# Two-layer conditioned residual block on one core: the first and the last linear stage take two chunks in a matmul of 512 columns

## The chip, the core and the metric

The kernel runs on one core of a Trainium2 chip. The metric is the device time of one execution in microseconds (us), lower is better. The engines that matter here are PE (TensorE, matmul), ACT (ScalarE), DVE (VectorE) and POOL (GpSimd); SP (SyncE) issues nearly all DMA transfers. Each engine works its own instructions strictly in the order of the program, and they wait for each other by semaphores alone.

## What is computed

`x` has 8 batches of 1024 tokens with 512 features, all in float32. Cut to what matters, with a style vector per batch (s0, sk, so) made from `cond_512` at the start:

```python
y  = ((x * s0) @ W0.T) * demod0 + b0          # layer L0, 512 x 512
x1 = x + clip(y, -256, 256)
kx = ((x1 * sk) @ Wk.T) * demodk + bk         # layer K
# attention of the 16 heads of one token with each other: a 16 x 16 matrix per token, q = k = v = kx
k  = kx.reshape(B, N, 16, 32)
A  = softmax(einsum('bnhd,bnjd->bnhj', k, k) / sqrt(32))
a  = einsum('bnhj,bnjd->bnhd', A, k).reshape(B, N, 512)
out = x1 + ((a * so) @ Wo.T) * demodo + bo    # layer O
```

## The kernel before

The 8192 tokens are cut into N = 32 chunks of T = 256 tokens. Features lie on the partitions (KB = 4 blocks of 128), tokens along the free axis. Everything is written out by hand in Bass: each engine's list of steps is a table, and the order in the table is the order of execution.

For a chunk c the steps are these. ACT and DVE split the scaled input into a high and a low part in fp32r (`x_hi_of` on ACT, 2 halves of 2 instructions; `x_lo_of` on DVE, the same). PE forms **L0** in 4 blocks m of 128 output features; each block is 12 matmuls (4 k, times w_hi·hi, w_hi·lo, w_lo·hi) into one of NLB = 4 PSUM banks. ACT evacuates a block (`l0_out`: demodulation and bias). DVE clips and adds x (`make_x1`, in halves). `x1_hi_of`, `x1_lo_of` split x1, PE forms **K**, `k_out` evacuates it to `kx`. SP writes kx to DRAM and reads it back turned (`k_to_dram`, then `k_from_dram`, 4 issues), DVE reorders it (`turn_k`, tile `k_rhs`), POOL (3 groups) and ACT (`copy_keys`) spread it into `k_bd`, and PE forms **scores**. For the values SP writes `k_rhs` to DRAM (`v_to_dram`) and reads it turned (`v_from_dram`, 4 issues, tile `k_v`); DVE transposes it (`turn_v`). Softmax alternates: ACT `even_scores`, DVE `merge_scores`, `subtract_maxima`, ACT `exponentials`, DVE `sums`, `normalise`; then DVE (`spread_probabilities`) and ACT (`spread_some`, 4 instructions) spread the probabilities and PE forms **pv**. ACT copies the result out of PSUM (`evacuate_y`), SP turns it through DRAM (`y_to_dram`, 4 issues, then `y_from_dram`, tile `yr`), ACT and DVE split it (`y_hi_of`, `y_lo_of`), PE forms **O**, ACT evacuates it (`o_out`), DVE adds x1 (`finish`), SP stores it (`store`).

The steps are software-pipelined. A head fills the pipeline (chunks 0 to 5), a loop runs i = 6 to 29, a tail empties it. In a turn of the loop PE does L0 of chunk i, O of i-4, K of i, pv of i-2 and scores of i-1, in this order (L179); ACT, DVE and SP have tables of their own for a turn (L654, L850, L341). A linear block waits for the evacuation of the block four before it (L414). SP's queue is in order too: a transfer that waits holds up all transfers behind it.

Of the kernel before, what the change touches and what calls it, by code (L numbers as in the profile page):

```python
# [34 lines left out]
def build(nc, xT, condT, wT, affT, aff_b, lin_b, block_ones, token_mask, head_diag, dim_eye, outT):  # L35
# [33 lines left out]
    with ExitStack() as ctx:  # L69
# [27 lines left out]
        x_hi, x_lo = sb("x_hi", [KB, T], F32R), sb("x_lo", [KB, T], F32R)  # L97
# [15 lines left out]
        y_hi, y_lo = sb("y_hi", [2, KB, T], F32R), sb("y_lo", [2, KB, T], F32R)  # L113
        o_sb = sb("o", [2, KB, T])
# [64 lines left out]
        def pe_steps(i):  # L179
            return blocks(L0, i) + blocks(O, i - 4) + blocks(K, i) + one("pv", i - 2) + one("scores", i - 1)  # L180
# [34 lines left out]
        def _(sp):  # L215
# [71 lines left out]
            def store(c, h, parts):  # L287
# [118 lines left out]
        def _(pe):  # L406
            operands = {L0: (x_hi, x_lo), K: (x1_hi, x1_lo)}
            split = {L0: (a_xhi, v_xlo), K: (a_x1hi, v_x1lo), O: (a_yhi, v_ylo)}

            def linear(l, c, m, width=1):  # L410
# [101 lines left out]
        def _(act):  # L512
            evacuated = []

            def evacuate(l, c, m, out):
# [21 lines left out]
            def x_hi_of(c, h):  # L537
# [4 lines left out]
                if c >= 2:  # L542
                    act.wait_ge(pe_lin, done(L0, c - 1 if c > 2 else 0, KB - 1))
                hi_part(L0, c, h, y_hi[:, 1] if c == 1 else x_hi, x_sb[:, c % 2], a_xhi)
# [387 lines left out]
```

## Time and profile before

| what | value |
|---|---|
| time, median of 3 runs (lowest, highest) | 707.4 us (705.88, 712.59) |
| the profiled execution | 707.48 us, of which its span is 705.6 us |
| busy in the span: PE / DVE / ACT / POOL | 690.7 / 580.8 / 545.0 / 116.3 us (98 / 82 / 77 / 16%) |
| chain that ended last, by engine | PE 76%, ACT 8%, DVE 7%, DMA 4%, issue 3%, SP 2% |
| DMA | 140.39 MB, mean 199 GB/s |

The page gives busy time by engine; the chain of waits says what the end of the span waited for; the timeline gives instructions with their start, so that the distance from one start to the next is what an instruction costs its engine when nothing waits. "Idle before" names the engine that ended a wait.

### The profile page before, as it was taken

The numbers are of one execution on the slowest core, as the hardware profiler recorded it, in microseconds if no ns is written. First come the engines' busy times: TensorE is split into PE (matmuls) and PEld (weight loads), VectorE is DVE, ScalarE is ACT, GpSimd is POOL, SyncE is SP. The second block draws the span as 40 slices with busy tenths as digits, with TensorE's granted clock in tenths as the row PEclk, the third lists the DMA queues.
The fourth block names the chain that finished last, engine by engine and source line by source line (L and its number), as shares of the span: only waits on it lengthen the run. The fifth ranks groups of instructions, "written<-read, shape, count | busy, mean of one in ns | idle before, by whom it ended". The sixth has DMA issues, their size and how long they took to land.

```text
span 705.6 us, 21755 instructions
## 1 busy us (share of the span) xinstructions
PE 690.7 (98%) x8944; PEld 674.6 (96%) x8944; DVE 580.8 (82%) x1048; ACT 545.0 (77%) x1072; POOL 116.3 (16%) x107
## 2 busy tenths in 40 slices
PE   9999999999999999999999999999999999999877
PEld 8999999999999999999999999999999999999877
DVE  4689988889888889988889878888988889878853
ACT  6898977888777888777787867788777788877743
POOL 2021301111101111110111101111110111112200
PEclk9999999999999999999999999999999999999989
DMA  8367867678877777886667785777876777878853
GB/s 294 126 181 199 218 184 198 193 210 212 210 186 199 201 205 223 214 213 182 190 201 207 209 227 133 206 203 215 217 205 173 208 200 206 210 188 220 218 155 120
DMA packets 229700, 140.39 MB, mean 199 GB/s; under 512 B 141281, under 2 KB 223201, under 8 KB 229601
## 3 DMA queue, kind: packets, MB, share of 16 engines
q1 hardware_dynamic: 228544, 138.73, 72.2%
q8 instruction: 71, 1.16, 0.7%
q10 hardware_dynamic: 1056, 0.26, 0.2%
q14 instruction: 29, 0.23, 0.1%
HBM read 71.85 MB, written 67.11 MB: 197 GB/s over the span
## 4 chain that ended last, share of the span: by engine, by line
PE 76%; ACT 8%; DVE 7%; DMA 4%; issue 3%; SPq 2%; POOL 0%; ACTq 0%; DVEq 0%
PE lin_ps L429 61%; PE y_ps L501 7%; PE s_ps L483 6%; ACT p_bd L628 2%; DMA yr<-y_turned 1%; ACT x_hi L534 1%; ACT kx L525 1%; ACT y_hi L534 1%; PE s_ps L439 1%; ACT o L525 1%; SPq L273 1%; DVE x L803 1%; DMA k_v<-v_turned 1%; DVE sc L833 1%; ACT sc L622 1%
## 5 line engine op out<-in xcount | busy, mean ns | idle before, releaser
L429 PE MATMUL lin_ps<-x_hi,w_hi 128*128 128x256 f32 x1008 | 286.4, 285 | 0.3
L429 PE MATMUL lin_ps<-x_lo,w_hi 128*128 128x256 f32 x1008 | 281.4, 280 | 0.9 <-issue 0.9
L429 PE MATMUL lin_ps<-x_hi,w_lo 128*128 128x256 f32 x1008 | 281.2, 280 | 0.0
L398 POOL COPY k_bd<-k_rhs 32x1024 f32<-32x1024 f32 x96 | 111.9, 1166 | 547.5 <-DVE k_rhs L782 543.8
L429 PEld LDWEIGHTS lin_ps<-x_hi,w_hi 128*128 128x128 f32 x1008 | 189.8, 189 | 8.4 <-issue 4.6
L429 PEld LDWEIGHTS lin_ps<-x_hi,w_lo 128*128 128x128 f32 x1008 | 189.9, 189 | 1.0 <-issue 1.0
L429 PEld LDWEIGHTS lin_ps<-x_lo,w_hi 128*128 128x128 f32 x1008 | 190.0, 189 | 0.0
L534 ACT ACTIVATE x_hi<-x,style 128x256 fp32r<-128x256 f32 x252 | 113.2, 501 | 61.2 <-DVE x L803 55.8
L725 DVE SCALAR_TENSOR_TENSOR x_lo<-x,style,x_hi 128x256 fp32r<-128x256 f32 x252 | 145.1, 627 | 12.5 <-ACT x_hi L534 12.5
L429 PE MATMUL lin_ps<-y_hi,w_hi 128*128 128x256 f32 x528 | 149.5, 283 | 1.0 <-ACT o L525 1.0
L429 PE MATMUL lin_ps<-y_lo,w_hi 128*128 128x256 f32 x528 | 148.7, 282 | 0.0
L429 PE MATMUL lin_ps<-y_hi,w_lo 128*128 128x256 f32 x528 | 148.6, 281 | 0.0
L429 PEld LDWEIGHTS lin_ps<-y_hi,w_hi 128*128 128x128 f32 x528 | 100.2, 190 | 2.4 <-ACT o L525 1.2
L429 PEld LDWEIGHTS lin_ps<-y_lo,w_hi 128*128 128x128 f32 x528 | 100.2, 190 | 0.0
L429 PEld LDWEIGHTS lin_ps<-y_hi,w_lo 128*128 128x128 f32 x528 | 100.2, 190 | 0.0
L628 ACT ACTIVATE p_bd<-p_turned,tok_mask 128x512 f32<-128x512 f32 x128 | 90.2, 715 | 7.9 <-DVE p_turned L839 7.9
L525 ACT ACTIVATE x<-lin_ps,bias,demod 128x256 f32<-128x256 f32 x128 | 68.4, 556 | 16.1 <-PE lin_ps L429 14.3
L525 ACT ACTIVATE o<-lin_ps,bias,demod 128x256 f32<-128x256 f32 x128 | 69.9, 555 | 12.5 <-PE lin_ps L429 12.2
L525 ACT ACTIVATE kx<-lin_ps,bias,demod 128x256 f32<-128x256 f32 x128 | 67.9, 556 | 5.4 <-PE lin_ps L429 4.6
L501 PE MATMUL y_ps<-p_bd,v 128*32 128x128 f32 x2048 | 64.1, 278 | 4.7 <-DVE p_bd L846 4.4
L483 PE MATMUL s_ps<-k_bd,k_rhs 128*32 128x128 f32 x2048 | 62.3, 273 | 2.8 <-issue 1.8
L501 PEld LDWEIGHTS y_ps<-p_bd,v 128*32 128x32 f32 x2048 | 55.9, 112 | 8.6 <-DVE p_bd L846 4.6
(63 smaller groups left out, 740.0 us busy)
## 6 DMA issues: line engine op xcount, KB each, us to landing
k_turned<-kx SPq DMA_DIRECT2D x32, 512.0 KB, 2.9
k_st<-k_turned SPq DMA_DIRECT2D x128, 128.0 KB, 3.2
v_turned<-k_rhs SPq DMA_DIRECT2D x32, 512.0 KB, 6.1
k_v<-v_turned SPq DMA_DIRECT2D x128, 128.0 KB, 3.5
y_turned<-y SPq DMA_DIRECT2D x126, 128.0 KB, 3.3
x<-xT SPq DMA_DIRECT2D x31, 512.0 KB, 5.7
yr<-y_turned SPq DMA_DIRECT2D x31, 512.0 KB, 4.6
outT<-o SPq DMA_DIRECT2D x31, 512.0 KB, 4.3
```

Of the source, the lines that this page charges most:

```text
L273: sp.dma_start(y_dram[c % 2].rearrange("(n d) t -> d n t", d=HD)[:, :, j * TB:(j + 1) * TB], y_sb[HD * j:HD * (j + 1), :, :, :].rearrange( ...
L398: pool.tensor_copy(k_bd[HD * r:HD * (r + 1), r], k_rhs[HD * r:HD * (r + 1)]).then_inc(g_kbd, 1)
L429: mm = pe.matmul(lin_ps[:, (n + j) % NLB, 0:T], w[:, k, (m + j) * P:(m + j + 1) * P], r[:, k, :], start=(q == 0), stop=(q == len(passes) - 1))
L439: pe.matmul(s_ps[:, 0, 0:P], idle, idle, start=True, stop=True)
L483: mm = pe.matmul(s_ps[HD * ct:HD * (ct + 1), x, q * P:(q + 1) * P], k_rhs[:, w:w + 2].rearrange("p w n -> p (w n)"), k_bd[:, :, w:w + 2].r ...
L501: mm = pe.matmul(y_ps[HD * j:HD * (j + 1), q // PB, (q % PB) * P:(q % PB + 1) * P], v_sb[:, c % 2, j * QS + q], p_bd[:, grp].rearrange("p ...
L525: act.activation(out, src, ACT.Identity, bias=bias_sb[l][:, m:m + 1], scale=demod[l][:, m, b:b + 1]).then_inc(a_lin, 1)
L534: a = act.activation(out[:, k], src[:, k], ACT.Copy, scale=style[l][:, k, b:b + 1])
L622: act.activation(sc[:], sc[:], ACT.Exp, scale=SCALE).then_inc(a_exp, 1)
L628: act.activation(p_bd[:, :, TG // 2 + t, :], p_turned[:], ACT.Copy, scale=tok_mask[:, TG // 2 + t:TG // 2 + t + 1]).then_inc(a_pbd, 1)
L725: v = dve.scalar_tensor_tensor(out=out[:, k], in0=src[:, k], scalar=style[l][:, k, b:b + 1], in1=hi[:, k], op0=ALU.mult, op1=ALU.subtract)
L803: dve.tensor_tensor(x1h, x1h, x_sb[:, c % 2, h * half:(h + 1) * half], ALU.add).then_inc(v_x1, 1)
```

## The change

In the loop, L0 and O take two chunks at once. A turn of the loop is now two chunks (i = 6, 8, ... 28), and the moving operand of their matmuls has 512 columns, which fills a PSUM bank. K, scores and pv stay one chunk at a time, twice in a turn. Head and tail keep single chunks, apart from a few steps moved over their border: scores(4) from the head into the first turn, the high and low part of x for chunk 7 into the head, scores(28) into the tail, and the turning of y(3), v(4) and one store ahead of the loop.

- The split tiles get the two chunks side by side (`x_hi`, `x_lo`, `y_hi`, `y_lo`: [KB, 2, T]).
- `linear_pair` (PE) waits at m = 0 for both chunks' parts in full. One signal is given for the pair.
- `l0_pair_out` (ACT) evacuates 512 columns in one instruction; `o_pair_out` evacuates them in two of 256.
- `make_x1_pair` (DVE) clips and adds one block m of both chunks, 512 columns, where `make_x1` took two blocks of one chunk; `finish_pair` likewise.
- `store_pair` (SP) stores two blocks of both chunks in one transfer; `store_pair(c, 1)` waits for all four `finish_pair`.
- PE's, ACT's, DVE's and SP's tables for a turn are new.

```diff
-        x_hi, x_lo = sb("x_hi", [KB, T], F32R), sb("x_lo", [KB, T], F32R)
+        x_hi, x_lo = sb("x_hi", [KB, 2, T], F32R), sb("x_lo", [KB, 2, T], F32R)
...
         def pe_steps(i):
-            return blocks(L0, i) + blocks(O, i - 4) + blocks(K, i) + one("pv", i - 2) + one("scores", i - 1)
+            return (pair(L0, i, [0, 1]) + one("scores", i - 2) + pair(L0, i, [2, 3]) + pair(O, i - 4, [0, 1])
+                    + one("scores", i - 1) + blocks(K, i) + one("pv", i - 2) + pair(O, i - 4, [2, 3])
+                    + one("pv", i - 1) + blocks(K, i + 1))
...
+            def store_pair(c, h):
+                ks = slice(h * KB // 2, (h + 1) * KB // 2)
+                sp.wait_ge(v_out, 2 * c + 2 * (h + 1))
+                sp.dma_start(outT_v[:, ks, c * T:(c + 2) * T], o_sb[:, ks].rearrange("p k c t -> p k (c t)")
+                             ).then_inc(st_o[h], DMA)
...
-            for i in range(FIRST_LOOP, last - 1):
+            for i in range(FIRST_LOOP, last - 1, 2):
                 k_to_dram(i - 1)
                 k_from_dram(i - 1)
-                v_from_dram(i - 2)
-                y_to_dram(i - 3)
-                store(i - 5, 0, 1)
-                y_from_dram(i - 3)
+                v_to_dram(i - 1)
+                v_from_dram(i - 1)
                 load_x(i + 2)
-                v_to_dram(i - 1)
+                load_x(i + 3)
+                store_pair(i - 4, 0)
+                k_to_dram(i)
+                y_to_dram(i - 2)
+                k_from_dram(i)
+                y_from_dram(i - 2)
+                v_to_dram(i)
+                store_pair(i - 4, 1)
+                y_to_dram(i - 1)
+                v_from_dram(i)
+                y_from_dram(i - 1)
...
+            def linear_pair(l, c, m):
+                n = block_no[(l, c, m)]
+                pe.wait_ge(a_lin, n - NLB + 1)
+                if m == 0:
+                    pe.wait_ge(split[l][0], 2 * (c + 2))
+                    pe.wait_ge(split[l][1], 2 * (c + 2))
...
+                    mm = pe.matmul(lin_ps[:, n % NLB, 0:2 * T], w[:, k, m * P:(m + 1) * P],
+                                   r[:, k].rearrange("p c t -> p (c t)"), start=(q == 0), stop=(q == len(passes) - 1))
+                mm.then_inc(pe_lin, 1)
...
             def act_steps(i):
+                    (i, l0_pair_out, 0), (i-3, y_hi_of, 0), (i-3, y_hi_of, 1), (i, l0_pair_out, 1),
...
+            def make_x1_pair(c, m):
+                x1m = x1_sb[:, c % NX1:c % NX1 + 2, m]
+                dve.wait_ge(a_lin, done(L0, c, m))
+                dve.tensor_scalar(x1m, x1m, CLAMP, -CLAMP, ALU.min, ALU.max).then_inc(v_clip, 1)
+                dve.wait_ge(v_clip, 2 * c + m + 1)
+                dve.tensor_tensor(x1m, x1m, x_sb[:, :, m], ALU.add).then_inc(v_x1, 1)
...
+            def finish_pair(c, m):
+                dve.wait_ge(a_lin, done(O, c, m))
+                dve.tensor_tensor(o_sb[:, m], o_sb[:, m], x1_sb[:, c % NX1:c % NX1 + 2, m], ALU.add).then_inc(v_out, 1)
...
             def dve_steps(i):
+                    (i-2, turn_v), (i, make_x1_pair, 0), (i-3, y_lo_of, 0), (i-3, y_lo_of, 1), (i, make_x1_pair, 1),
```

SP's queue before, one whole turn of the loop (one chunk); L291 is the store, L284 `y_from_dram`, L273 `y_to_dram`:

```order
L240 DMA k_turned<-kx 128x4x256 [waits k_in_landed,a_lin]
L249 DMA k_st<-k_turned 32x16x64 [waits v_krhs,k_out_landed]
L249 DMA k_st<-k_turned 32x16x64 x3
L265 DMA k_v<-v_turned 32x4x256 [waits v_v,v_out_landed]
L265 DMA k_v<-v_turned 32x4x256 x3
L273 DMA y_turned<-y 32x16x64 [waits y_in_landed,a_y]
L273 DMA y_turned<-y 32x16x64 x3
L291 DMA outT<-o 128x4x256 [waits v_out]
L284 DMA yr<-y_turned 128x4x256 [waits v_ylo,a_yhi,y_out_landed]
L223 DMA x<-xT 128x4x256 [waits v_x1]
L257 DMA v_turned<-k_rhs 128x1024 [waits v_in_landed,v_krhs]
```

SP's queue now, from the end of one turn into the next (the turn ends behind the first `yr` row that follows `k_v`):

```order
L287 DMA v_turned<-k_rhs 128x1024 [waits v_in_landed,v_krhs]
L327 DMA outT<-o 128x2x512 [waits v_out]
L303 DMA y_turned<-y 32x16x64 [waits y_in_landed,a_y]
L303 DMA y_turned<-y 32x16x64 x3
L295 DMA k_v<-v_turned 32x4x256 [waits v_v,v_out_landed]
L295 DMA k_v<-v_turned 32x4x256 x3
L314 DMA yr<-y_turned 128x4x256 [waits v_ylo,a_yhi,y_out_landed]
L270 DMA k_turned<-kx 128x4x256 [waits k_in_landed,a_lin]
L279 DMA k_st<-k_turned 32x16x64 [waits v_krhs,k_out_landed]
L279 DMA k_st<-k_turned 32x16x64 x3
```

Before, the store stood behind `y_turned` and ahead of `yr`; now the second store of the pair stands ahead of `y_turned`, `k_v` and `yr` of the second chunk, and the next turn's K transfers come behind all of them.

DVE before, from `turn_k` (L782) over the turn's end to the next turn's `merge_scores` (L808); the `x_lo` row is `x_lo_of`, the `o` row `finish`:

```order
L782 COPY k_rhs<-k_st 128x1024
L793 STREAM_TRANSPOSE v<-k_v 128x512 x2
L725 SCALAR_TENSOR_TENSOR x_lo<-x,style,x_hi 128x256 x4
L822 TENSOR_TENSOR o<-o,x 128x512 x2
L725 SCALAR_TENSOR_TENSOR y_lo<-yr,style,y_hi 128x256 x4
L808 SCALAR_TENSOR_TENSOR sc<-s_ps,odd_mask,sc 128x512
```

DVE now, from the second `turn_k` of a turn (L864) to the first of the next; the turn ends behind the first `y_lo` row:

```order
L864 COPY k_rhs<-k_st 128x1024
L808 SCALAR_TENSOR_TENSOR x_lo<-x,style,x_hi 128x256 x4
L917 TENSOR_TENSOR o<-o,x 128x512
L808 SCALAR_TENSOR_TENSOR y_lo<-yr,style,y_hi 128x256 x4
L875 STREAM_TRANSPOSE v<-k_v 128x512 x2
L891 TENSOR_SCALAR x<-x 128x2x256
L893 TENSOR_TENSOR x<-x 128x2x256
L808 SCALAR_TENSOR_TENSOR y_lo<-yr,style,y_hi 128x256 x4
L891 TENSOR_SCALAR x<-x 128x2x256
L893 TENSOR_TENSOR x<-x 128x2x256
L864 COPY k_rhs<-k_st 128x1024
```

The last `finish_pair` of a pair (the `o` row) now stands behind `turn_k` and four `x_lo`, and `turn_v` stands at the head of the turn, ahead of all of `make_x1_pair`.

ACT now, from the last two evacuations of K in one turn into the next turn; L588 is an evacuation, L664 `even_scores`, L700 `copy_keys`:

```order
L588 ACTIVATE kx<-lin_ps,bias,demod 128x256 x2
L588 ACTIVATE x<-lin_ps,bias,demod 128x2x256
L598 ACTIVATE y_hi<-yr,style 128x256 x4
L588 ACTIVATE x<-lin_ps,bias,demod 128x2x256
L664 ACTIVATE sc<-s_ps,odd_mask 128x512
L700 ACTIVATE k_bd<-k_rhs 32x1024
L588 ACTIVATE x<-lin_ps,bias,demod 128x2x256
L598 ACTIVATE x_hi<-x,style 128x256 x2
L686 ACTIVATE sc<-sc 128x512
```

ACT before, from the second last evacuations of K in one turn into the next:

```order
L534 ACTIVATE y_hi<-yr,style 128x256 x2
L525 ACTIVATE kx<-lin_ps,bias,demod 128x256
L534 ACTIVATE y_hi<-yr,style 128x256 x2
L525 ACTIVATE kx<-lin_ps,bias,demod 128x256 x2
L607 ACTIVATE y<-y_ps 128x16x32 x2
L600 ACTIVATE sc<-s_ps,odd_mask 128x512
L525 ACTIVATE x<-lin_ps,bias,demod 128x256
L622 ACTIVATE sc<-sc 128x512
L525 ACTIVATE x<-lin_ps,bias,demod 128x256 x2
```

The `y_hi` of the pair's second chunk, which stood among the `kx` of the turn's end before, now stands behind the first L0 evacuation of the next turn, and `copy_keys` stands ahead of the third.

## Rows read from the trace of the kernel before

**Rows 1.** Busy time in stretches (busy us, instructions, granted clock, DMA share, GB/s)
```profile
321.60:342.40 20.80, 20.80 (x275) 20.47 (x273) 18.12 (x34) 16.60 (x34) 3.48 (x3) 1.00 0.74 204
407.10:410.10 3.00, 3.00 (x15) 3.00 (x15) 2.04 (x3) 0.76 (x2) 0.00 (x0) 0.52 0.43 120
```

**Rows 2.** Chain that ended last, one turn: start us, us, what
```profile
338.77 1.89 PE y_ps L501 x64
340.66 1.75 PE s_ps L483 x64
```

**Rows 3.** Timeline of PE: start, us, line, operation; x_hi at 301 is L0
```profile
301.03 0.28 PE L429 MATMUL lin_ps<-x_lo,w_hi 128*128 128x256 f32 x1
...
306.40 0.28 PE L429 MATMUL lin_ps<-x_hi,w_lo 128*128 128x256 f32 x1
...
406.77 0.41 PE L483 MATMUL s_ps<-k_bd,k_rhs 128*32 128x128 f32 x2 [1.77 <-issue]
```

**Rows 4.** Timeline of SP's queue, one turn: start, duration of the issues
```profile
321.44 0.36 SPq L240 DMA_DIRECT2D k_turned<-kx  x1
324.36 1.91 SPq L249 DMA_DIRECT2D k_st<-k_turned  x4
326.37 1.86 SPq L265 DMA_DIRECT2D k_v<-v_turned  x4
328.33 2.79 SPq L273 DMA_DIRECT2D y_turned<-y  x4
331.17 0.80 SPq L291 DMA_DIRECT2D outT<-o  x1
333.78 0.38 SPq L284 DMA_DIRECT2D yr<-y_turned  x1
```

**Rows 5.** DMA issues of the page: count, KB each, median us to landing
```profile
k_st<-k_turned SPq DMA_DIRECT2D x128, 128.0 KB, 3.2
v_turned<-k_rhs SPq DMA_DIRECT2D x32, 512.0 KB, 6.1
...
yr<-y_turned SPq DMA_DIRECT2D x31, 512.0 KB, 4.6
```

**Rows 6.** Line 265, `v_from_dram`: ns of an issue and us to landing, min/median/max
```profile
L265 SPq DMA_DIRECT2D k_v<-v_turned x128: 302/432/2033, 49.4 to 667.8; - x128
...
DMA to landing us min/median/max: 2.7/3.5/5.9
```

**Rows 7.** Timeline of ACT, the same turn
```profile
321.32 1.07 ACT L607 ACTIVATE y<-y_ps 128x512 f32<-128x512 f32 x2
...
333.01 0.71 ACT L628 ACTIVATE p_bd<-p_turned,tok_mask 128x512 f32<-128x512 f32 x1
333.63 0.89 ACT L534 ACTIVATE x_hi<-x,style 128x256 fp32r<-128x256 f32 x2
334.43 0.54 ACT L525 ACTIVATE o<-lin_ps,bias,demod 128x256 f32<-128x256 f32 x1
...
337.48 1.06 ACT L636 ACTIVATE k_bd<-k_rhs 32x1024 f32<-32x1024 f32 x1
```

**Rows 8.** Timeline of DVE, the same turn
```profile
327.43 0.68 DVE L827 TENSOR_REDUCE total<-sc 128x32 f32<-128x512 f32 x1
...
328.53 0.69 DVE L833 TENSOR_TENSOR sc<-sc,rcp 128x512 f32<-128x512 f32 x1
...
329.99 0.38 DVE L801 TENSOR_SCALAR x<-x 128x512 f32<-128x512 f32 x1
...
331.02 0.87 DVE L725 SCALAR_TENSOR_TENSOR x_lo<-x,style,x_hi 128x256 fp32r<-128x256 f32 x2
...
334.46 1.10 DVE L782 COPY k_rhs<-k_st 128x1024 f32<-128x1024 f32 x1
```

**Rows 9.** Timeline of POOL, and of DVE beside it
```profile
335.62 3.60 POOL L398 COPY k_bd<-k_rhs 32x1024 f32<-32x1024 f32 x3 [17.08 <-DVE k_rhs L782]
...
336.70 3.20 DVE L725 SCALAR_TENSOR_TENSOR x_lo<-x,style,x_hi 128x256 fp32r<-128x256 f32 x4
```

More of the change, by code:

```diff
@@ L168, in blocks, with pair, l0_paired, o_paired @@
             return [("lin", l, c, m) for m in ms]
+        def pair(l, c, ms=range(KB)):
+            return [("pair", l, c, m) for m in ms]
+        def l0_paired(c):
+            return FIRST_LOOP <= c < last - 1
+        def o_paired(c):
+            return l0_paired(c + DEPTH)
+        def x1_made(c, h):
+            return 2 * (c - c % 2) + 2 * (h + 1) if l0_paired(c) else 2 * c + h + 1
+        def out_made(c):
+            return 2 * (c - c % 2) + KB if o_paired(c) else 2 * c + 2
         def one(step, c):
@@ L406, in _ @@
         def _(pe):
-            operands = {L0: (x_hi, x_lo), K: (x1_hi, x1_lo)}
+            operands = {L0: (x_hi, x_lo), K: (x1_hi, x1_lo), O: (y_hi, y_lo)}
             split = {L0: (a_xhi, v_xlo), K: (a_x1hi, v_x1lo), O: (a_yhi, v_ylo)}
@@ L414, in linear @@
                     pe.wait_ge(a_lin, n - NLB + 1)
-                borrowed = l == O or (l, c) == (L0, 1)
-                hi, lo = (y_hi[:, c % 2], y_lo[:, c % 2]) if borrowed else operands[l]
+                hi, lo = operands[l] if l == K else [t[:, :, c % 2] for t in operands[l]]
                 passes = [(k, w, r) for k in range(KB)
@@ L542, in x_hi_of @@
                 if c >= 2:
[L543 to L544 removed]
+                    act.wait_ge(pe_lin, done(L0, c - 2, KB - 1))
+                hi_part(L0, c, h, x_hi[:, :, c % 2], x_sb[:, c % 2], a_xhi)
             def weights_hi(l, h):
@@ L650, in o_out, with o_pair_out @@
                     act.wait_ge(st_o[c % 2], DMA * (c // 2))
-                evacuate(O, c, m, o_sb[:, c % 2, m].rearrange("p (l j s) -> p j l s", l=2, j=4))
+                    act.wait_ge(st_o[1], DMA * (last // 2 - 2))
+                evacuate(O, c, m, by_group(m, c % 2))
+            def o_pair_out(c, m):
+                if m == 0:
+                    for h in range(2):
+                        act.wait_ge(st_o[h], DMA * (c // 2))
+                evacuate(O, c, m, by_group(m, 0), by_group(m, 1))
@@ new lines, in act_steps @@
+                    (i-2, even_scores), (i-1, copy_keys), (i, l0_pair_out, 2), (i, x1_hi_of, 0), (i-2, exponentials),
+                    (i, l0_pair_out, 3), (i, x1_hi_of, 1), (i-4, o_pair_out, 0), (i-4, o_pair_out, 1),
+                    (i-2, spread_some, 0), (i-1, even_scores), (i-2, spread_some, 1), (i-2, spread_some, 2),
+                    (i-2, spread_some, 3), (i, k_out, 0), (i + 2, x_hi_of, 0), (i + 2, x_hi_of, 1), (i, k_out, 1),
+                    (i-1, exponentials), (i, k_out, 2), (i + 3, x_hi_of, 0), (i + 3, x_hi_of, 1), (i, k_out, 3),
@@ L713, in _ @@
                 (last, o_out, 2), (last, o_out, 3)]
-            for c, step, *args in act_head + [s for i in range(FIRST_LOOP, last - 1) for s in act_steps(i)] + act_tail:
+            for c, step, *args in act_head + [s for i in range(FIRST_LOOP, last - 1, 2) for s in act_steps(i)] + act_tail:
                 step(c, *args)
@@ L729, in x_lo_of @@
             def x_lo_of(c, h):
-                hi, lo = (y_hi[:, 1], y_lo[:, 1]) if c == 1 else (x_hi, x_lo)
-                lo_part(L0, c, h, lo, x_sb[:, c % 2], hi, a_xhi, v_xlo)
+                lo_part(L0, c, h, x_lo[:, :, c % 2], x_sb[:, c % 2], x_hi[:, :, c % 2], a_xhi, v_xlo)
             def x1_lo_of(c, h):
@@ L890, in _ @@
                 (last - 1, finish, 1), (last, finish, 0), (last, finish, 1)]
-            for c, step, *args in dve_head + [s for i in range(FIRST_LOOP, last - 1) for s in dve_steps(i)] + dve_tail:
+            for c, step, *args in dve_head + [s for i in range(FIRST_LOOP, last - 1, 2) for s in dve_steps(i)] + dve_tail:
                 step(c, *args)
```

136 lines of the change are left out of this document (79 added, 57 removed).

## Prediction

> **What bounds the kernel now.** I read busy time in stretches first. In a turn of the loop (one chunk, 20.8 us) PE is busy in all 20.80 us, DVE in 18.12, ACT in 16.60 [rows 1]: PE sets the pace. Then PE's timeline: the 2nd to the 48th matmul of an L0 stage start within 5.37 us, 116.7 ns apart [rows 3], while 256 columns at 2.4 GHz are 106.7 ns. So 10 ns of each are not streaming. How a longer stream behaves is shown where the granted clock was 0.52, the level of 1.2 GHz, after a gap of 1.77 us in PE's issue [rows 1, 3]: of the 15 records there one is the end of a scores step, 14 matmuls in 3.0 us are 214 ns each, and 256/1.2 is 213.3. With a stream that long the 10 ns are gone.
>
> **What the change takes from PE.** In the loop 96 matmuls of 512 columns a turn (two chunks) replace 192 of 256. No row shows one at full clock; the bounds are 213.3 ns (no loss, as at the low clock) and 223.4 (the 10 ns stay). I take 218. A turn of PE is then 96 x 0.218 = 20.9, K 96 x 0.1167 = 11.2, two pv 3.8, two scores 3.5 [rows 2]: 39.4 us against 41.6, so -2.2 us a turn and -26 over 12 turns, if PE stays the bound.
>
> **What it adds: a ring through SP, DVE and ACT.** DVE's work is the same number of instructions of 512 or 256 elements, 2 x 18.12 = 36.2 us a turn. ACT saves four evacuations. What is new is the order. I call F the end of the last `finish_pair` of a turn.
>
> *Part 1, SP and DMA.* The second `store_pair` waits for F, and behind it in SP's queue stand `y_to_dram`, `v_from_dram`, `y_from_dram` of the second chunk and the next turn's `k_to_dram`, `k_from_dram`. From F on [rows 4, 5]: store 0.8; y issues and landing 5.45 (328.33 to 333.78); `yr` issue 0.4; `k_turned` issue to landing 2.9 (321.44 to 324.36); the fourth `k_st` is issued 1.4 later and lands after 3.2. So `turn_k` can start at F+14.2. On the way the last `k_v` lands at F+0.8+2.8+1.4+3.5 = F+8.5 [rows 4, 6] and `yr` at F+0.8+5.45+4.6 = F+10.9. `turn_v` is the first step of DVE's new turn and `y_hi` the second of ACT's, so both engines stand still till then: DVE does 1.7 us of `y_lo` after F (twice the 0.87 of two [rows 8]) and waits until F+8.5; ACT waits until F+10.9, does y_hi, an evacuation and `even_scores`, and waits in `copy_keys` for `turn_k`. Between F+10.9 and F+14.2 DVE finishes `make_x1_pair` 0 and 1 and `y_lo`, just in time.
>
> *Part 2, ACT.* `turn_k` takes 1.05. From `copy_keys` to the `x1_hi` of the turn's second chunk ACT has, by the distance of starts [rows 7]: copy 1.05; 8 half splits (x1, x of two chunks, x1) at 0.80, 6.4; 8 `spread_some` at 0.62, 5.0; 6 halves of O and 4 of K at 0.5, 5.0; two L0 evacuations of 512 columns; `evacuate_y` 1.0; `even_scores` and `exponentials`, as wide as `spread_some`, 1.2. The 512-column evacuation has no row: it costs at least the 0.5 of one with 256 and at most the 0.71 of a 512-wide SBUF pass; I take 0.6, 1.2 for two. Sum 20.9. ACT waits twice in it for DVE. After `turn_k` DVE does three score-wide operations (0.68 as the first of `sums`, with the step between 0.72; 2.2), `make_x1_pair` 1.03, `x1_lo` 0.85, `make_x1_pair` 1.03 [rows 8], 5.1 in all, while ACT gets there after 3.65: 1.5. Then `sums` 1.1, `x1_lo` 0.85, `normalise` 1.46 before `spread_some` can start: 0.6.
>
> *Part 3, DVE.* After that `x1_hi`: `x1_lo` 0.85, `x_lo` of the next chunk 1.7, `finish_pair` 0.6 (an add: 1.03 less the clip's 0.42), `turn_k` 1.05, four `x_lo` beside POOL 3.2 [rows 9], `finish_pair` 0.6: 8.0, and that is the next F.
>
> The ring: 14.2 + 1.05 + 20.9 + 2.1 + 8.0 + about 0.7 for seven hand-overs (`turn_k` ends at 335.56, POOL starts at 335.62: 0.06 to 0.1 each) = 46.9 us a turn against 41.6. PE is done with its turn in 39.4 and waits the rest, most of it ahead of the second pv (its `spread_some` ends only about 38 us after L0's start) and ahead of O for `y_lo`. The first turn has the same lags, since the head issues y(3), store(1), v(4), yr(3) in the same order when pv(3) ends.
>
> **Sum.** The profiled execution is 707.48 us (span 705.6 and 1.9 around it), equal to the median of the runs. 12 turns x (46.9 - 41.6) = +63.6. PE's own gap and slow stretch in the loop (1.77 and 14 x 0.1 = 1.4) now lie inside PE's waiting: -3. Head and tail exchange one scores step for another: 0. Predicted 768 us.
>
> **Bounds.** Of the landings on the ring (y, `k_turned`, `k_st`) each may be 0.8 shorter, as 2.7 is to 3.5 for `k_v` [rows 6], and each of the 8 issues (4 y, 4 k) 0.1 shorter: 43.7 a turn. Upward: `load_x` stands behind `v_from_dram`, which waits for `v_turned`. If that lands after 6.1 as now [rows 5] (with two other transfers beside it; here it is alone), ACT waits 1.6 for x: 48.5. So 730 to 787 for this case; rounded outward for small errors, 728 to 790.
>
> **POOL beside DVE.** Four `x_lo` that start while POOL copies `k_rhs` take 3.20 us [rows 9], against 2 x 0.87 without [rows 8]: POOL's copies cost DVE about 1.5. After the first `turn_k` of a new turn it is the subtraction of the maxima and `make_x1_pair` that run beside POOL; no row shows these there. I bound their loss by 0 and by the same 1.5 and take 0. The Trainium skill, "SBUF — State Buffer", section "Who interferes with whom", says that a VectorE instruction with two SBUF inputs and a GpSimd instruction that reads SBUF exclude each other for a whole instruction. By that rule the subtraction and the adds are held up too, and the upper bound holds: 12 x 1.5 = 18 us more, about 786. The rows on `x_lo` agree with it; for the adds no row does.
>
> **Rivals.**
> - *DVE alone sets the pace.* ACT's hand-overs always come early enough, and only the gap at `turn_v` counts: 36.2 + 8.5 - 1.7 = 43.0 a turn, 707.5 + 17 - 3 = 721 us. For it: DVE has the most work next to PE. Against it: ACT cannot start `copy_keys` before F+15.3, and 21 us of queue stand behind it.
> - *PE stays the bound, faster.* 39.4 a turn: 681 us. It decides at DVE's gap: DVE has 41.6 - 36.2 = 5.4 us of free time in two old turns, and the gap after F takes 6.8. With the shortest issues and landings of line 265 (0.3 and 2.7) for all, F to `k_v` is 0.3 + 7 x 0.3 + 2.7 = 5.1 and the gap 3.4; only then, and if `yr` and `k_st` also come that fast, does the saving of PE appear. For it: these minima were measured. Against it: they would have to come in every turn, while stores, y, `k_v`, `yr`, k all start in the same 14 us.
> - *Slower still.* The loss beside POOL and the wait for x come together: 46.9 + 1.5 + 1.6 = 50.0 a turn, 805 us.
> - *A pair's matmul costs as much as two* (233 ns): PE's turn is 40.9, still under the ring, and nothing else moves. It has no case of its own.
>
> A slow stretch of PE's clock after its new waits (1.4 us each by the low-clock rows [rows 1]) delays K of the second chunk; the ring does not pass through it.
>
> **How the numbers follow.** The ring as worked out (728 to 790): 0.60. DVE alone (706 to 728): 0.17. PE bound (under 706): 0.09. Slower still (790 to 815): 0.14. The predicted time is the ring's, 768. The range reaches from 712, which takes in 0.12 of the second case, to 806, which takes in 0.09 of the last: 0.81. A measurement of this kernel can tell about 1% from no change: faster by that is under 700 (PE bound, 0.08), within it 700 to 714 (its upper end and the lower end of DVE alone, 0.05), slower the rest, 0.87.
>
> **What would show it.** Matmuls of 512 columns 213 to 223 ns apart; if not, PE's term is wrong. Turns of about 47 us in the loop, L0 to second L0. DVE's `v` group (`turn_v`) with a wait of some 7 us a turn that `k_v`'s landing ends, and ACT's `y_hi` or its neighbours waiting for `yr` till about 11 us behind F; if these waits are short, the ring is wrong. In SP's queue `outT` waiting for DVE's o, with `y_turned` directly behind it. PE idle about 7 us a turn, released by ACT's `p_bd` at pv and by DVE's `y_lo` at O. If turns are near 43 and ACT idles ahead of `spread_some`, DVE alone was right; at 39.4 with PE without idle time, the rival that ends faster.

## The result and the profile after

The changed kernel takes 850.7 us (median of 4 runs, 848.65 to 855.43) against 707.9 for the kernel before beside it (705.88 to 712.59): a ratio of 1.205, with an interval of 1.199 to 1.210. It is slower, as predicted, but by 143 us where the prediction had 61, and outside the range of 712 to 806.

The loss lies in the loop. From one start of L0 to the next a turn takes 53.8 us on average (11 distances, 52.5 to 55.9), where two turns before took 2 x 20.8 [rows 1]. From the first L0 of the loop to the first start behind it are 645 us now and 504 before: 141 of the 143 us. The page of the profile after:

```profile
span 849.0 us, 19307 instructions
...
PE 738.3 (87%) x7792; PEld 644.1 (76%) x7792; DVE 590.2 (70%) x1048; ACT 527.9 (62%) x1024; POOL 115.8 (14%) x107
...
DVE 28%; DMA 23%; SPq 16%; ACT 15%; PE 11%; issue 6%; ACTq 0%; DVEq 0%
```

PE fell from 98% of the span to 87%, and in the chain that ended last (third row) it fell from 76% to 11%. DMA, SP's queue, DVE and ACT now share the chain: the path goes round through all of them. One turn in stretches (columns as in rows 1: time, then busy us and number of instructions of PE, PE's weight loads, DVE, ACT and POOL, then granted clock, DMA share, GB/s), then the waits of the engines (total us, times, longest):

```profile
220.33:273.12 52.79, 46.06 (x448) 38.78 (x449) 36.80 (x65) 31.35 (x63) 6.92 (x6) 0.94 0.56 160
```

```profile
...
ACT y_hi L598 <- DMA yr<-y_turned: 103.0, 15, 11.1
DVE v L875 <- DMA k_v<-v_turned: 102.9, 13, 10.2
ACT k_bd L700 <- DVE k_rhs L864: 70.6, 23, 5.1
...
DVE k_rhs L864 <- DMA k_st<-k_turned: 45.8, 26, 3.2
```

DVE works 36.8 us in the turn, as much as in two turns before (2 x 18.12), and ACT 31.4. Each stands still for most of the rest: DVE at `turn_v` some 8 us a turn, ACT at `y_hi` as long and once more at `copy_keys` (`k_bd`). PE's granted clock is 0.94 here where it was 1.00, but PE's matmuls are only about 4% of the chain of this turn, so its clock is hardly what the turn waits for. SP's queue from F on, the end of the last `finish_pair` (start, duration of the issues; the counterpart of [rows 4]):

```profile
220.81 0.38 SPq L327 DMA_DIRECT2D outT<-o  x1
221.29 3.06 SPq L303 DMA_DIRECT2D y_turned<-y  x4
224.75 2.08 SPq L295 DMA_DIRECT2D k_v<-v_turned  x4
227.37 0.38 SPq L314 DMA_DIRECT2D yr<-y_turned  x1
227.84 0.45 SPq L270 DMA_DIRECT2D k_turned<-kx  x1
233.83 1.91 SPq L279 DMA_DIRECT2D k_st<-k_turned  x4
```

The same turn on DVE, and POOL's copies:

```profile
220.10 0.68 DVE L917 TENSOR_TENSOR o<-o,x 128x512 f32<-128x512 f32 x1
...
229.66 1.30 DVE L875 STREAM_TRANSPOSE v<-k_v 128x512 f32<-128x512 f32 x2 [7.29 <-DMA k_v<-v_turned]
...
238.71 1.09 DVE L864 COPY k_rhs<-k_st 128x1024 f32<-128x1024 f32 x1 [2.48 <-DMA k_st<-k_turned]
...
241.22 1.32 DVE L905 TENSOR_TENSOR sc<-sc,mx 128x512 f32<-128x512 f32 x1
242.46 1.26 DVE L891 TENSOR_SCALAR x<-x 128x512 f32<-128x512 f32 x1
...
264.26 2.46 DVE L808 SCALAR_TENSOR_TENSOR x_lo<-x,style,x_hi 128x256 fp32r<-128x256 f32 x6 [3.27 <-ACT x_hi L598]
...
267.95 1.10 DVE L864 COPY k_rhs<-k_st 128x1024 f32<-128x1024 f32 x1 [0.63 <-DMA k_st<-k_turned]
268.96 4.01 DVE L808 SCALAR_TENSOR_TENSOR x_lo<-x,style,x_hi 128x256 fp32r<-128x256 f32 x4
272.90 0.68 DVE L917 TENSOR_TENSOR o<-o,x 128x512 f32<-128x512 f32 x1
```

```profile
239.87 3.57 POOL L443 COPY k_bd<-k_rhs 32x1024 f32<-32x1024 f32 x3 [19.96 <-DVE k_rhs L864]
269.11 3.59 POOL L443 COPY k_bd<-k_rhs 32x1024 f32<-32x1024 f32 x3 [25.68 <-DVE k_rhs L864]
```

This is the predicted ring with its steps in the predicted places: the store directly behind F, `turn_v` waiting for `k_v`, `turn_k` at the end of the K transfers, ACT's chain, the last `x_lo`, the next F at 273.58. Its terms are longer, however, and one wait comes in that the prediction did not have:

| part of the ring (this turn) | predicted, us | measured, us |
|---|---|---|
| F (220.78) to `turn_k` (238.71) | 14.2 | 17.9 |
| `turn_k` to the pair's last `x1_hi` (DVE's `x1_lo` follows at 264.26) | 24.1 | 25.6 |
| from there to the next F (273.58) | 8.0 | 9.3 |
| hand-overs, counted apart | 0.7 | in the rows above |
| sum | 46.9 | 52.8 |

In the first part `k_turned` took 6.0 us from issue to the first `k_st` instead of 2.9 and y took 6.1 instead of 5.45. In the others DVE's steps beside POOL grew: subtraction 1.32, clip 1.26, four `x_lo` 4.01. And in the third part the second `turn_k` (267.95) does not follow the `finish_pair` ahead of it at once, but stands 0.63 us for its own `k_st`. The chain of this turn reaches it through SP's queue a second time, over `evacuate_y` (ACT `y`), the four issues of `y_to_dram` (L303) and the K transfers behind them (start, us, what):

```profile
258.68 0.60 ACT y L671
...
259.30 0.32 SPq L303
...
262.08 0.73 SPq L279
...
264.21 3.72 DMA k_st<-k_turned
...
267.95 1.10 DVE k_rhs L864
```

In all 12 turns this wait is there, 0.5 to 2.1 us, 1.1 on average.

The matmuls of pairs, PE's timeline at L0 (start, us):

```profile
220.63 0.40 PE L489 MATMUL lin_ps<-x_lo,w_hi 128*128 128x512 f32 x1
220.87 0.40 PE L489 MATMUL lin_ps<-x_hi,w_lo 128*128 128x512 f32 x1
221.10 0.39 PE L489 MATMUL lin_ps<-x_hi,w_hi 128*128 128x512 f32 x1
```

They start 234 ns apart (the median over the loop too), twice the 116.7 of 256 columns [rows 3]. PE has nothing from the width.

### The profile page after: what moved, and what is told of

Read it like the earlier page. It is cut to its first block, busy times and chain, and to the rows that moved or that the text cites. A ratio compares the mean times of both kernels' runs of the same rounds, so it can differ in the third digit from the quotient of the medians.

```text
span 849.0 us, 19307 instructions
## 1 busy us (share of the span) xinstructions
PE 738.3 (87%) x7792; PEld 644.1 (76%) x7792; DVE 590.2 (70%) x1048; ACT 527.9 (62%) x1024; POOL 115.8 (14%) x107
## 4 chain that ended last, share of the span: by engine, by line
DVE 28%; DMA 23%; SPq 16%; ACT 15%; PE 11%; issue 6%; ACTq 0%; DVEq 0%
DMA k_st<-k_turned 11%; DMA k_turned<-kx 9%; PE lin_ps L473 9%; DVE x_lo L808 8%; SPq L303 7%; ACT x_hi L598 5%; SPq L279 5%; DVE k_rhs L864 3%; ACT kx L588 3%; ACT p_bd L692 3%; SPq L295 3%; DVE sc L905 2%; DVE x L891 2%; DVE x L893 2%; DVE mx L903 1%
## 5 line engine op out<-in xcount | busy, mean ns | idle before, releaser
L473 PE MATMUL lin_ps<-x_hi,w_hi 128*128 128x256 f32 x640 | 190.7, 299 | 19.6 <-DVE x_lo L808 17.5
L473 PE MATMUL lin_ps<-x_lo,w_hi 128*128 128x256 f32 x640 | 184.8, 290 | 0.0
L473 PE MATMUL lin_ps<-x_hi,w_lo 128*128 128x256 f32 x640 | 184.4, 289 | 0.0
L808 DVE SCALAR_TENSOR_TENSOR x_lo<-x,style,x_hi 128x256 fp32r<-128x256 f32 x256 | 137.1, 591 | 49.6 <-ACT x_hi L598 49.6
L473 PEld LDWEIGHTS lin_ps<-x_hi,w_hi 128*128 128x128 f32 x640 | 127.5, 200 | 30.9 <-issue 30.7
L473 PEld LDWEIGHTS lin_ps<-x_lo,w_hi 128*128 128x128 f32 x640 | 127.5, 200 | 0.0
L473 PEld LDWEIGHTS lin_ps<-x_hi,w_lo 128*128 128x128 f32 x640 | 126.9, 199 | 0.0
L489 PE MATMUL lin_ps<-y_hi,w_hi 128*128 128x512 f32 x192 | 80.5, 419 | 20.9 <-DVE y_lo L808 20.9
L489 PE MATMUL lin_ps<-x_hi,w_hi 128*128 128x512 f32 x192 | 79.9, 416 | 18.6 <-DVE x_lo L808 18.3
L542 PEld LDWEIGHTS s_ps<-k_bd,k_rhs 128*32 128x32 f32 x2048 | 58.0, 115 | 34.7 <-POOL k_bd L443 29.3
L489 PE MATMUL lin_ps<-y_lo,w_hi 128*128 128x512 f32 x192 | 78.0, 406 | 0.0
L588 ACT ACTIVATE kx<-lin_ps,bias,demod 128x256 f32<-128x256 f32 x128 | 69.5, 557 | 13.7 <-PE lin_ps L473 13.2
L700 ACT ACTIVATE k_bd<-k_rhs 32x1024 f32<-32x1024 f32 x32 | 33.8, 1057 | 70.8 <-DVE k_rhs L864 70.6
L588 ACT ACTIVATE x<-lin_ps,bias,demod 128x512 f32<-128x512 f32 (+1 forms) x80 | 53.8, 686 | 38.6 <-PE lin_ps L489 36.1
```

The lines of the kernel that those rows point to most:

```text
L489: mm = pe.matmul(lin_ps[:, n % NLB, 0:2 * T], w[:, k, m * P:(m + 1) * P], r[:, k].rearrange("p c t -> p (c t)"), start=(q == 0), stop=(q = ...
L542: mm = pe.matmul(s_ps[HD * ct:HD * (ct + 1), x, q * P:(q + 1) * P], k_rhs[:, w:w + 2].rearrange("p w n -> p (w n)"), k_bd[:, :, w:w + 2].r ...
L588: a = act.activation(out, src, ACT.Identity, bias=bias_sb[l][:, m:m + 1], scale=demod[l][:, m, b:b + 1])
L808: v = dve.scalar_tensor_tensor(out=out[:, k], in0=src[:, k], scalar=style[l][:, k, b:b + 1], in1=hi[:, k], op0=ALU.mult, op1=ALU.subtract)
```

## The experiments

In what follows the kernel before beside each group of runs took 705.7 to 708.0 us. "The change" is the kernel just described. Each time is that of one run; the four runs of the change lie within 0.8%.

**Does the width matter at all?** Each matmul of 512 columns is made two of 256:

```diff
-                for q, (k, w, r) in enumerate(passes):
-                    mm = pe.matmul(lin_ps[:, n % NLB, 0:2 * T], w[:, k, m * P:(m + 1) * P],
-                                   r[:, k].rearrange("p c t -> p (c t)"), ...)
+                for u in range(2):
+                    for q, (k, w, r) in enumerate(passes):
+                        mm = pe.matmul(lin_ps[:, n % NLB, u * T:(u + 1) * T], w[:, k, m * P:(m + 1) * P],
+                                       r[:, k, u], ...)
```

> Edit: each matmul of 512 columns is made as two of 256 into the two halves of the same bank; all orders, signals and waits stay. Theory: the width gives PE nothing (512 columns start 233.4 ns apart in the changed kernel, twice the 116.7 of 256 before), and PE is not what a turn waits for: the total stays within 1%, 842 to 859 us, with PE's matmul time in the loop the same to 2%. Rival (the wide matmul saves weight loads and the loss of time would be larger without it): 20 us or more slower, 870 us.

857.8 us, within the range of the theory; PE was busy for 741.4 us against 738.3, and the matmuls of 256 start 117 ns apart. The width is worth 7 us at most here; neither the loss nor a gain comes from it.

**What a matmul costs by its width.** The kernel before with six bursts of 24 matmuls put at PE's end:

```diff
+            for width in (128, 256, 384, 512):
+                for q in range(24):
+                    pe.matmul(y_ps[:, 0, 0:width], w_hi[L0][:, q % KB, 0:P], w_hi[K][:, q % KB, 0:width], ...)
+            for width in (256, 512):
+                for q in range(24):
+                    pe.matmul(y_ps[:, 0, 0:width], wb[:, :], xb[:, 0:width], ...)
```

> The kernel before with six bursts of 24 matmuls behind its last block, which write PSUM that nobody reads: moving operand fp32r with 128, 256, 384 and 512 columns, then bf16 with 256 and 512. Each has its own weights of 128 columns. Theory (fp32r streams at a lower rate than one column a cycle at the clock of 2.4 GHz: 256 in 116.7, 512 in 233.4 ns): 384 columns take 175 ns, 128 not less than 58 (or the weight load, about 110), and bf16 streams at 2.4 GHz: 512 in 213 to 217 ns. Rival (a fixed 10 ns for a matmul of 256 and a different one for 512): 384 columns 170 ns, and bf16 the same 233 ns for 512.

The distance of starts (median) is 111, 120, 173 and 227 ns for fp32r, 109 and 216 for bf16, all at a granted clock of 1.00: the 173 of 384 columns lie between the two theories, the 216 of bf16 is the first one's. The groups of lines (busy us; only 23 of the last burst are recorded):

```profile
L514 PE MATMUL y_ps<-w_hi 128*128 128x512 f32 x24 | 5.6, 391 | 0.0
L518 PE MATMUL y_ps<-xb,wb 128*128 128x512 bf16 x23 | 5.1, 379 | 0.1
...
L514 PE MATMUL y_ps<-w_hi 128*128 128x256 f32 x24 | 3.1, 285 | 0.0
```

Against the columns at 2.4 GHz (106.7, 160, 213.3) fp32r loses 13 to 14 ns at 256, 384 and 512 columns alike, bf16 2 to 3. In a quiet burst the loss is therefore one of each instruction, as the prediction read it from [rows 3], and a pair would save it once. In the kernel it does not: 116.7 ns lose 10 and 234 lose 21. The bursts differ from the kernel in their operands, in what the other engines do beside them, and in that no sum runs over several matmuls; which of these counts was not separated. The Trainium skill, "TensorE: Matmul & The Clock Gate", section "Back-to-back issue gap", gives N/2.4 + 2.5 ns for an isolated matmul, by which 512 columns are an estimated 215.8 ns: bf16 agrees, in a burst (216); fp32r does not, neither in the burst nor in the kernel. The same section gives about 131 ns for 512 columns in a stream of weight loads and matmuls; no run here shows that, and the bursts, which are such streams, decide for 216 and 227.

**Is it the store ahead of y?** SP's queue alone: the second store goes behind `y_from_dram(i - 1)`.

```diff
-                store_pair(i - 4, 1)
                 y_to_dram(i - 1)
                 v_from_dram(i)
                 y_from_dram(i - 1)
+                store_pair(i - 4, 1)
```

> Edit: in SP's queue the second store of the pair moves from ahead of y_to_dram, v_from_dram and y_from_dram of the second chunk to behind them; nothing else changes. Theory (the ring through SP: the turn is as long as the way from the last finish_pair through these transfers and back): y_to_dram then starts when v_to_dram has been issued, about 269.4 in the turn that starts at 220.33, instead of 274.1, so a turn falls from 53.5 us by 4 to 5 us, the total to 790 to 803 us. Rival (the transfers are slow because they are bunched, whatever their order; or DVE's and ACT's queues alone set the turn): the turn stays at 52 to 54 us, 840 to 855 us.

806.8 us, 44 less, and 4 us above the ring's range; a turn is 50.7 us. The place of the wait for F in the queue is a cause. What the move did not mend stands in the same stretch of SP's queue:

```profile
420.23 0.38 SPq L314 DMA_DIRECT2D yr<-y_turned  x1
420.65 0.51 SPq L327 DMA_DIRECT2D outT<-o  x1
421.25 0.41 SPq L270 DMA_DIRECT2D k_turned<-kx  x1
428.31 1.91 SPq L279 DMA_DIRECT2D k_st<-k_turned  x4
```

`k_turned` takes 7.06 us there, and 6.8 on average over the loop; `yr` and the store stand directly ahead of it.

**The same from the other end.** DVE's table alone: the last `finish_pair` ahead of `turn_k` and the four `x_lo`.

```diff
-                    (i-4, finish_pair, 2), (i, turn_k), (i + 3, x_lo_of, 0), (i + 3, x_lo_of, 1),
-                    (i-4, finish_pair, 3), (i-2, y_lo_of, 0), (i-2, y_lo_of, 1)]
+                    (i-4, finish_pair, 2), (i-4, finish_pair, 3), (i, turn_k), (i + 3, x_lo_of, 0), (i + 3, x_lo_of, 1),
+                    (i-2, y_lo_of, 0), (i-2, y_lo_of, 1)]
```

> DVE's last finish_pair of a turn moves ahead of turn_k(i) and the four x_lo; no other step moves. Ring theory: F, the end of that step, comes about 5 us earlier in a turn (1.0 for turn_k, 4.0 for the four x_lo beside POOL), the store and all that stands behind it in SP's queue with it, so a turn is 3.5 to 4.5 us shorter: 12 x 4 = 48, so 795 to 812 us, the same gain as the run with the store behind y_from_dram. Rival (the place of F in DVE's order does not matter, ACT's own order sets the turn): 840 to 855.

815.2 us: 3 us above the range named, 25 below the rival's. A turn is 50.8 us. An earlier F pulls the whole turn forward by 3.0 us, so the ring runs through F.

**Is it DVE's gap at `turn_v`?** `turn_v` goes from the head of DVE's turn to just ahead of `normalise`.

```diff
-                    (i-2, turn_v), (i, make_x1_pair, 0), ...
+                    (i, make_x1_pair, 0), ...
-                    ... (i, x1_lo_of, 1), (i-2, normalise),
+                    ... (i, x1_lo_of, 1), (i-2, turn_v), (i-2, normalise),
```

> Edit: in DVE's table for a turn, turn_v of chunk i-2 moves from the head of the turn to just ahead of normalise of i-2. DVE's wait for k_v, 102.9 us in the whole run, goes. Theory (ring; turn_k and y_hi wait for later landings of the same SP queue, and DVE catches up before them): the turn changes by less than 1.5 us, total 833 to 855 us. Rival (DVE's standstill at turn_v sets the turn): 6 to 7 us a turn come back, 765 to 785 us.

904.4 us, a turn of 58.2 instead of 53.8; both theories missed. The gap only moved: DVE now waits 107 us for `y_hi`. And a new one came up, since `v_from_dram` of the next chunk waits for `turn_v` and stands ahead of `load_x` in SP's queue: ACT waits 38 us for x, where in the change it waited only 5.4, at the start of the run.

```profile
DVE y_lo L808 <- ACT y_hi L598: 107.1, 14, 11.5
ACT y_hi L598 <- DMA yr<-y_turned: 104.5, 13, 11.8
...
PE y_ps L560 <- ACT p_bd L692: 59.4, 13, 5.1
...
ACT x_hi L598 <- DMA x<-xT: 38.4, 13, 5.9
```

So one of the two longest waits of DVE and ACT was no free time waiting to be used: with it taken away `yr` and `turn_k` are waited for as before. That the wait for x is what made the turn longer is likely, but was not tested by itself.

**What holds `k_turned`?** Over the loop the time from its issue to the first `k_st` is 6.4 us on average (12 turns, 5.1 to 7.8), and 3.15 before the change (the 24 issues between 112 and 617 us, 20 of them 2.9 to 3.1). Two transfers issued just ahead of it are cut to a quarter of their rows, first `yr`, then `k_v`, then both; issues and waits are unchanged.

```diff
...
+                    if FIRST_LOOP <= c + 1 < last:
+                        ks = slice(0, 1)
                     sp.dma_start(yr_sb[:, ks], ...)
...
+                    rs = slice(0, 1 if FIRST_LOOP <= c + 1 < last else R)
-                    sp.dma_start(k_v[HD * ct:HD * (ct + 1)]..., src[:, :, ct])
+                    sp.dma_start(k_v[HD * ct:HD * (ct + 1), rs]..., src[:, rs, ct])
```

> The change with the transfer yr of the loop cut to a quarter of its rows (the rest of yr stays as it was before). In the trace of the change k_turned, issued right behind yr and the four k_v, takes 5.1 to 7.8 us until the first k_st can be issued, mean 6.4, against 2.9 where it runs alone before the change. Theory A (yr, 512 KB as large as k_turned, takes half of what the transfers move): 6.4 falls to 3.5 to 4.5 us, and the turn by 2 to 3 us: 815 to 830 us. Theory B (the four k_v ahead, of many small packets, are what k_turned shares with): stays at 5.5 to 6.5, 840 to 852 us. Theory C (it is something else, such as k_turned's own writes): stays at 6.4, no change.

> The change with the four transfers k_v of the loop cut to a quarter of their rows; issues and waits as in the change. Theory A (yr is what delays k_turned): 6.4 us stays within 0.5, and the run gains only from k_v's earlier landing, 840 to 852 us. Theory B (k_v): 6.4 falls to 3.5 to 4.5 us, 815 to 830 us.

> Both cuts together. If it is these two beside it that hold k_turned, 6.4 us falls to 2.9 to 3.5, the value of before, and the turn by 3 to 3.5 us: 805 to 818 us. Rival (the store outT of 512 KB and y, or k_turned's own packets): it stays above 4.5 us, and the run above 820.

| cut | `k_turned` to first `k_st`, mean (lowest, highest), us | time, us |
|---|---|---|
| none | 6.4 (5.1, 7.8) | 850.7 |
| `yr` | 4.4 (3.6, 5.3) | 817.8 |
| `k_v` | 5.4 (5.0, 6.6) | 841.7 |
| both | 3.7 (3.0, 5.3) | 815.8 |

Of the 3.5 us above 2.9 `yr` takes 2.0 and `k_v` 1.0 (theory A left at most 0.5 for it), both together 2.7. The other 0.8 is not explained, and 3.7 lies above the 2.9 to 3.5 expected. By time the three runs lie in the ranges of theory A, theory A and the first theory. With both short `k_turned` takes 2.99 to 3.06 us in seven of 13 records, one of them here, behind a `yr` of a quarter:

```profile
174.36 0.36 SPq L317 DMA_DIRECT2D yr<-y_turned  x1
174.82 0.38 SPq L270 DMA_DIRECT2D k_turned<-kx  x1
177.81 1.92 SPq L279 DMA_DIRECT2D k_st<-k_turned  x4
```

So most of the loss of `k_turned` is its neighbours'. With `yr` cut the run falls by 2.7 us a turn (33/12), more than the 2.0 of `k_turned` alone; the rest may be the earlier `y_hi` or `k_st`, which these runs don't separate.

**Are DVE's steps beside POOL on the ring?** POOL's copies are cut to an eighth, so that the scores lack most keys:

```diff
-                    pool.tensor_copy(k_bd[HD * r:HD * (r + 1), r], k_rhs[HD * r:HD * (r + 1)]).then_inc(g_kbd, 1)
+                    pool.tensor_copy(k_bd[HD * r:HD * (r + 1), r, 0:4], k_rhs[HD * r:HD * (r + 1), 0:4]).then_inc(g_kbd, 1)
```

> The change with GpSimd's copies of k_bd cut to an eighth (4 of 32 rows of keys each; the scores then lack most keys); no other instruction differs. Theory that these copies hold up DVE and that this lies on the ring: in the trace of the change a turn has a subtraction of 1.32 us against 0.69, a clip of 1.26 against 0.42 and four x_lo of 4.01 against 1.66 beside them, 3.8 us in all; 12 x 3.8 = 46, so 800 to 812 us. If only the later group counts (the first is covered by ACT's own chain), 2.35 x 12 = 28: 818 to 828. Rival (DVE's long steps come from something else, such as transfers into SBUF, or they lie off the path): 840 to 855.

804.2 us: 46.5 less, the 46 of the theory. The steps are back at their lengths alone:

```profile
234.74 0.69 DVE L905 TENSOR_TENSOR sc<-sc,mx 128x512 f32<-128x512 f32 x1
235.35 0.42 DVE L891 TENSOR_SCALAR x<-x 128x512 f32<-128x512 f32 x1
...
260.94 1.68 DVE L808 SCALAR_TENSOR_TENSOR x_lo<-x,style,x_hi 128x256 fp32r<-128x256 f32 x4
```

**Can the order alone bring the turn back to PE's bound?** First SP's queue in a new order, then ACT's and DVE's tables too:

```diff
-            y_from_dram(3)
             for i in range(FIRST_LOOP, last - 1, 2):
                 k_to_dram(i - 1)
+                y_from_dram(i - 3)
                 k_from_dram(i - 1)
+                if i > FIRST_LOOP:
+                    store_pair(i - 6, 1)
...
-                store_pair(i - 4, 1)
                 y_to_dram(i - 1)
                 v_from_dram(i)
-                y_from_dram(i - 1)
...
```

> SP's queue alone is put in another order: the transfers of k come ahead of the store and of yr, and y_from_dram of the second chunk goes to the next turn, behind k_to_dram; DVE and ACT are as in the change. Ring theory: turn_k no longer waits behind y, yr and store, so its wait goes from F+17.9 to the time at which v's path and ACT end, and the run is 2 to 3 us a turn below the run with the store alone behind (807): 765 to 785 us. Rival 1 (the engines' own orders, ACT's chain above all, bind as soon as the store is out of the way): 795 to 810. Rival 2 (the transfers run beside one another and a first place in the queue is worth nothing): 800 to 850.

> The queue order as in the run before, and in ACT's and DVE's tables the steps that wait for a transfer (turn_v, turn_k, y_hi, copy_keys) stand behind work that is ready. If the loss is the order alone, as the ring theory has it, the turn is bounded by PE's 41.1 us (a pair's matmul at 234 ns) and DVE's 37: 41 to 44 us a turn, 700 to 735 us. Rival (there is a loss in the pairs themselves: buffers too few for two chunks in flight, so that a wait appears at another place whatever the order): above 760.

In the second, `turn_v` stands behind the first `make_x1_pair`, `turn_k(i-1)` behind `subtract_maxima`, `y_hi(i-3)` behind the second L0 evacuation and `copy_keys(i-1)` behind the fourth; some steps around them change places too. The queue alone gives 774.6 us (47.7 a turn), as expected; with the tables 750.2 (45.7 a turn), between the two theories. The second with POOL's copies cut as above:

> The kernel with queue and both tables reordered, with the same cut copies of k_bd. Its turn is 45.7 us. DVE's steps beside the copies are 4.6 us a turn longer there (add 1.41 against 0.69, two x_lo 2.43 against 0.88 and 1.66 against 0.88, add 1.52 against 0.69, four y_lo 2.44 against 1.68). Theory that this is what keeps it above PE's 41.1: 41.1 to 42 us a turn, 695 to 712 us. Rival (what is left there is the wait for yr, 3 us a turn in ACT, which the copies don't change): 735 to 750.

724.5 us, between the two theories, and 43.4 a turn (42.9 without the first): POOL was half of what was left, not all of it. Two turns of that run (columns as in rows 1):

```profile
301.24:343.75 42.51, 42.09 (x450) 35.75 (x449) 33.46 (x66) 32.16 (x65) 2.72 (x6) 1.00 0.71 202
343.75:385.74 41.99, 41.99 (x450) 35.84 (x449) 32.57 (x64) 30.05 (x59) 2.72 (x6) 1.00 0.70 193
```

Here PE is busy in all but 0.4 us of a turn, as before the change, and the turn is 42.0 to 42.5 us, no shorter than two old ones (41.6). In such turns pairs end where single chunks were, so the buffers of the pairs are no bound of their own above that. Of the orders that were run and leave nothing out, the best (750.2) is 43 us behind the kernel before.

## Why the prediction was right in direction and wrong in size

- **The ring: right, but for one crossing (below).** Each of its stations is in the trace, and the runs that shorten it at four places (the queue, F, the transfers, DVE's steps beside POOL) each shorten the run. PE idles and the engines wait where it said. *DVE alone* is refuted by the turn of 53.8 us and by the moved `turn_v`, which should have helped it. *PE stays the bound* fell with 87% of the span.
- **The step that failed is part 1's `k_turned`**, 2.9 us from issue to landing. That row was a transfer with no other on the way (`v_turned`, the last one ahead of it, had landed), and the prediction itself put it 0.4 us behind `yr` and close behind four `k_v`. It measured 6.4 on average, the largest single miss of the sum, and the runs with short neighbours show why for 2.7 of the 3.5 us. The bounds gave every landing a way down (0.8 shorter each) and only one a way up (`load_x`, which did not wait in the loop). The Trainium skill, "DMA: Bandwidth & Descriptors", section "Issuing engines are not separate DMA queues", says that DMAs run on the same 16 DMA engines and interleave, whichever engine issued them. By it a landing measured alone is only a lower bound, and the trace agrees with 6.4 against 2.9.
- **POOL beside DVE: sized at 1.5 us a turn, measured 3.8.** The 1.5 are inside the 3.2 that the prediction took for four `x_lo`. The subtraction and the clip it gave 1.5 at most and set to 0; they lost 1.5 (0.63 and 0.84). The other 0.8 is in the `x_lo`, 4.01 instead of 3.20. In [rows 9] they start 1.1 us behind POOL and two of the four are long; here `x_lo` stands directly behind `turn_k`, which releases POOL, and three of the four take 1.26. Without the copies all four take 1.7. The rule of the Trainium skill that the prediction weighed ("SBUF — State Buffer", section "Who interferes with whom") speaks for the loss, and the trace agrees for the subtraction and the `x_lo`. The adds that it was also applied to started behind the copies and took their 0.69; the clip has one SBUF input, and the rule as it was put has nothing on it.
- **A wait that the sum left out.** Part 3 lets the second `turn_k` follow `finish_pair` at once. But `y_to_dram` of the pair's first chunk waits for `evacuate_y` and stands ahead of `k_from_dram`, so the ring crosses SP's queue twice. By the trace this costs the 1.1 us a turn that DVE stands ahead of the second `turn_k`; no run was made for it.
- **Together.** On the turn shown: +3.7 in part 1, +1.5 in part 2 and +1.3 in part 3, less the 0.7 of hand-overs, which lie in the rows: 46.9 + 5.8 = 52.7 for 52.8. The remaining 1.0 to the mean of 53.8 is half part 1 (18.5 on average instead of 17.9), half the wait ahead of the second `turn_k` (1.1 instead of 0.6). *Slower still* named the loss beside POOL and gave it 1.5; its other half, the wait for x, never came.
- **PE's term: wrong, hidden.** 218 ns was taken for 512 columns on the ground that the 10 ns are lost once per instruction or less; the bursts bear that out (227 against 2 x 120), the kernel doesn't. The rival *costs as much as two* (233) is what was measured there, 234. PE's turn is then 96 x 0.016 = 1.5 us longer than in the sum. The lower bound, no loss at all, came from rows at the low clock, where 512 columns lose nothing either (427 ns, below); at full clock they lose 21. The saving of 2.2 us a turn was also set against the wrong figure: the same terms give 40.9 us for two old turns (192 x 0.1167 in place of 20.9), not 41.6, so even 218 ns would have saved only 1.5. Under the ring all this changed no time, but there was no saving to be hidden either: the 26 us that part promised, and with them the 681 us of the fast rival, did not exist.

Left open: why 512 columns lose twice what 256 do in the kernel and not in a burst, and what holds the reordered kernel, POOL's copies cut, at 43.4 us on average when single turns run at PE's 42.0; ACT still waits 53 us in that run for `yr`, and in the chain of one of its turns (343 to 386 us) `yr`, the issues of `y_to_dram` and `k_st` make 38%. No run put the neighbours of `k_turned` and POOL's copies right together. Whether the transfers can be spread over the turn without a loss elsewhere was not tried.

## What to carry to other kernels

When a longer loop turn is written out in one order, follow each engine's queue across the turn's border first: one waiting store ahead of others ties the end of a turn to its beginning, and the sum of that ring, not the busiest engine, is the turn. A duration read where a step runs alone is the lower end for a place where it gets neighbours; ask for each step of the ring which transfers are issued in the microseconds ahead of it and whether DVE's step now starts with POOL's. Before counting on wider matmuls, measure the distance of starts at both widths inside the kernel, in the type that is used.

## What the runs showed of the hardware beyond that

- fp32r is slower than its columns at full clock, bf16 hardly: 234 ns for 512 in the kernel, 227 in the burst, 216 in bf16. At a granted clock of 0.50 the kernel's 512 columns start every 427 ns, which is 512/1.2, with nothing lost (start, us):

```profile
132.09 0.63 PE L489 MATMUL lin_ps<-y_hi,w_lo 128*128 128x512 f32 x1
132.52 0.63 PE L489 MATMUL lin_ps<-y_hi,w_hi 128*128 128x512 f32 x1
```

- A DVE step that meets one of POOL's copies ends just behind that copy: in the turn shown the clip and the three long `x_lo` end 0.28 us behind the end of the copy that was running, the subtraction 0.55 behind it. So 0.42 becomes 1.26 and 0.69 becomes 1.32, while a copy takes 1.0 to 1.4 us. This fits a step that stands until the running copy ends, and not one that goes on at a share of its speed; it is read from the trace, and no run was made for it.
